# GpSimd sums the degrees of the first two pairs, pair 0 is loaded and multiplied tile by tile, the features come in six parts, and ScalarE's two loads of a piece stand apart

## What is computed

```python
h = jnp.maximum(_layernorm(x, axis=-1), 0.0)
x = x + _L0_gnn_ref(h, adj)      # (adj.T @ h) / adj.sum(axis=0)[:, None], 0 where the sum is 0
h = jnp.maximum(_layernorm(x, axis=-1), 0.0)
x = x + _L1_gnn_ref(h, adj, L1_gnn_W, L1_gnn_b)

def _L1_gnn_ref(x, adj, W, b):
    neigh1 = adj @ x
    x1 = jax.nn.swish(neigh1 @ W + b)
    neigh2 = adj @ x1
    return jax.nn.swish(neigh2 @ W + b)
```

## Time and profile before

| | us |
|---|---|
| median of 3 runs | 626.46 |
| lowest and highest run | 625.41, 627.19 |
| the profiled execution | 627.91 |
| its span in the profile | 626.1 |

### The profile page before, as it was taken

How to read it: one execution, slowest core, us unless ns; L and a number is a source line. 1 busy time by engine, 2 the same in 40 slices (tenths; PEclk the granted TensorE clock), 3 DMA queues, 4 the chain that set the end, 5 groups by cost and what they waited for, 6 DMA issues and landing times.

```text
span 626.1 us, 6939 instructions
## 1 busy us (share of the span) xinstructions
PE 609.1 (97%) x2296; PEld 413.3 (66%) x2296; DVE 541.8 (87%) x558; ACT 345.8 (55%) x456; POOL 544.2 (87%) x281
## 2 busy tenths in 40 slices
PE   8888999999999999999999999999999999999996
PEld 5355666577565567667667667777677677677774
DVE  5899699787868999897998998997998998998991
ACT  2493686595263354756656646646555546456551
POOL 2499799599688588999999989997999999998991
PEclk9999999999999999999999999999999999999999
DMA  9998999889999899999999999909999999999961
GB/s 324 382 372 301 339 320 358 293 329 275 353 351 367 287 345 334 347 347 347 347 347 348 347 348 347 283 25 220 308 348 349 348 349 348 348 348 349 348 176 34
DMA packets 151492, 197.73 MB, mean 316 GB/s; under 512 B 5280, under 2 KB 134560, under 8 KB 151456
## 3 DMA queue, kind: packets, MB, share of 16 engines
q1 hardware_dynamic: 86176, 132.92, 63.9%
...
## 4 chain that ended last, share of the span: by engine, by line
PE 63%; POOL 10%; DMA 9%; issue 6%; DVE 6%; ACT 3%; ACTq 2%; SPq 1%; POOLq 0%; DVEq 0%
PE dg L444 14%; PE dg L461 11%; PE dg L451 11%; PE dg L450 11%; DMA raw<-in_adj_dram 9%; PE m_ps L367 7%; POOL a_lo L855 5%; POOL at_lo L203 3%; PE m_ps L372 2%; PE m_ps L387 2%; PE m_ps L373 2%; DVE dg L699 2%; PE m_ps L474 2%; ACTq L285 2%; DVE turned L744 2%
## 5 line engine op out<-in xcount | busy, mean ns | idle before, releaser
L203 POOL TENSOR_TENSOR at_lo<-turned,at_hi 128x1024 fp32r<-128x1024 f32 x152 | 358.9, 2402 | 26.5 <-ACT at_hi L584 26.4
L744 DVE STREAM_TRANSPOSE turned<-raw 128x1024 f32<-128x1024 f32 x216 | 257.7, 1221 | 20.2 <-PE dg L461 13.9
L584 ACT ACTIVATE at_hi<-turned 128x1024 fp32r<-128x1024 f32 x152 | 157.0, 1055 | 97.8 <-DVE turned L744 71.1
L855 POOL TENSOR_TENSOR a_lo<-raw,a_hi 128x1024 fp32r<-128x1024 f32 x62 | 145.9, 2391 | 21.7 <-ACT a_hi L542 21.6
L699 DVE TENSOR_TENSOR dg<-raw,dg 128x2048 f32<-128x2048 f32 x60 | 137.5, 2291 | 29.2 <-DMA raw<-in_adj_dram 27.6
L450 PE MATMUL dg<-at_hi,f_hi 128*128 128x512 f32 x384 | 152.4, 397 | 0.3 <-ACT at_hi L584 0.2
L451 PE MATMUL dg<-at_hi,f_lo 128*128 128x512 f32 x384 | 151.3, 394 | 0.0
L461 PE MATMUL dg<-at_lo,f_hi 128*128 128x512 f32 x384 | 145.1, 459 | 1.2 <-POOL at_lo L203 1.2
L444 PE MATMUL dg<-turned,f_w 128*128 128x512 f32 x256 | 120.2, 592 | 0.0
L367 PE MATMUL m_ps<-raw,h 128*128 128x512 f32 x264 | 117.8, 593 | 2.5 <-DMA raw<-in_adj_dram 1.7
L461 PEld LDWEIGHTS dg<-at_lo,f_hi 128*128 128x128 f32 x384 | 72.1, 188 | 43.3 <-issue 28.9
...
## 6 DMA issues: line engine op xcount, KB each, us to landing
...
```

The lines of the kernel that those rows point to most:

```text
L203: return eng.tensor_tensor(at_lo[:, place(unit)], turned_tile(unit), at_hi[:, ring3(s)].bitcast(f32), ALU.subtract)
L584: act.activation(at_hi[:, ring3(s)], turned_tile(unit), ACT.Copy).then_inc(hi3_done, 1)
L744: dve.transpose(dst, src).then_inc(t3_done, 1)
L855: pool.tensor_tensor(a_lo[:, s % RING1], raw1[:, v % RAW1, i], a_hi[:, s % RING1].bitcast(f32), ALU.subtract).then_inc(lo1_done, 1)
```

## The change

Four things, apart from renumbering:

- **Degrees.** DVE no longer adds pairs 0 and 1. POOL sums their four tiles in `msgT`, an SBUF tile that is free then (`pool_degrees`: one instruction of 128x1024 for pair 0, two for pair 1). DVE starts with a copy of pair 2, and adds POOL's sum in `sum_degrees(0)` (one more instruction of 128x1024). ACT's first `copy_message`, which writes `msgT`, waits for that.
- **Pair 0** is loaded as two tiles of 512 KB with a semaphore each, and PE multiplies the first tile for both halves, then the second (`first_pair`).
- **Features** come in six parts of 2, 2, 4, 8, 8 and 8 tiles, ahead of the two tiles of pair 0 and of pairs 1, 3, 5 and 7. POOL's scale and shift of the last part stands behind its first `lo1`. With it, pair 8 becomes whole in quarter 0 (`WHOLE1_FIRST`), and its row pair one of those whose low part is made late.
- **ACT's blocks.** The second block of a piece is issued two units after the first.

```diff
-HEAD = ((0, 4), (4, 8), (8, 16), (16, 32))
-HEAD_PAIRS = (0, 2, 3, 4)
+HEAD = ((0, 2), (2, 4), (4, 8), (8, 16), (16, 24), (24, 32))
+HEAD_PAIRS = (0, 0, 1, 3, 5, 7)
+POOL_PAIRS = (0, 1)
-WHOLE1_FIRST = (0, 1, 2, 3, 4, 5, 7, 10, 13, 15)
-LATE_ROWS = (2, 3, 5)
-SPLIT_ROWS = (6, 8, 9, 11, 12, 14) + LATE_ROWS
+WHOLE1_FIRST = (0, 1, 2, 3, 4, 5, 7, 8, 10, 13, 15)
+LATE_ROWS = (2, 3, 5, 8)
+SPLIT_ROWS = (6, 9, 11, 12, 14) + LATE_ROWS
...
@@ SP
-                    sp.wait_ge(deg_added, back + 1)
+                    if back in POOL_PAIRS:
+                        sp.wait_ge(deg_pooled, 2 * back + 1)
+                    else:
+                        sp.wait_ge(deg_added, back + 1)
...
+            for i, ready in enumerate((tile0_loaded, raw1_loaded[0])):
+                load_head(i)
+                sp.dma_start(raw1[:, 0, i], adj_tiles[:, i, 0:QC]).then_inc(ready, 16)
+            for v in range(1, QUARTERS * PAIRS):
+                for b in head_parts(v):
+                    load_head(b)
                 load1(v)
...
@@ PE
+            def first_pair():
+
+                for i, ready in enumerate((tile0_loaded, raw1_loaded[0])):
+                    pe.wait_ge(ready, 16)
+                    pe.wait_ge(h_ready, i + 1)
+                    for half in range(2):
+                        cols = slice(half * 512, (half + 1) * 512)
+                        mm = pe.matmul(m_ps[:, cols], h[:, i], raw1[:, 0, i, cols], start=i == 0, stop=False)
+                mm.then_inc(main1_done, 1)
...
@@ ACT
                 act.wait_ge(half_done, q + 1)
+                if q == 0:
+
+                    act.wait_ge(degs_half, 1)
...
-                if unit == 1:
-                    load3(act, 3, ACT_BLOCKS)
-                if unit % QU == 0 and RAW3 <= i < len(PIECES) and i not in KEPT:
-                    load3(act, i, ACT_BLOCKS)
+                if unit in (1, 3):
+                    load3(act, 3, ACT_BLOCKS[unit // 2:unit // 2 + 1])
+
+                if unit % QU in (0, 2) and RAW3 <= i < len(PIECES) and i not in KEPT:
+                    load3(act, i, ACT_BLOCKS[unit % QU // 2:unit % QU // 2 + 1])
...
@@ DVE
-                if v % PAIRS == 0:
-                    if v > 0:
-                        dve.wait_ge(degs_ready, v // PAIRS)
+                if v == len(POOL_PAIRS):
+
+                    dve.tensor_copy(dg[:, :, :], src).then_inc(deg_added, len(POOL_PAIRS) + 1)
+                elif v % PAIRS == 0:
+                    dve.wait_ge(degs_ready, v // PAIRS)
...
+                if q == 0:
+                    dve.wait_ge(deg_pooled, 2 * len(POOL_PAIRS) - 1)
+                    step(dve.tensor_tensor(dg[:, 0, :], msgT[:, :], dg[:, 0, :], ALU.add))
...
-            head(0)
+            for b in head_parts(0):
+                head(b)
             for v in range(QUARTERS * PAIRS):
-                add_degrees(v)
-                if v < len(HEAD) - 1:
-                    head(v + 1)
+                if v not in POOL_PAIRS:
+                    add_degrees(v)
+                for b in head_parts(v + 1):
+                    head(b)
...
@@ POOL
+            def pool_degrees(v):
+
+                pool.wait_ge(raw1_loaded[v], 16)
+                if v == 0:
+                    pool.wait_ge(tile0_loaded, 16)
+                    pool.tensor_tensor(msgT[:, :], raw1[:, 0, 0], raw1[:, 0, 1], ALU.add).then_inc(deg_pooled, 1)
+                else:
+                    for i in range(2):
+                        pool.wait_ge(deg_pooled, 2 * v + i - 1)
+                        pool.tensor_tensor(msgT[:, :], raw1[:, v, i], msgT[:, :], ALU.add).then_inc(deg_pooled, 1)
+
-            for b, (lo, hi) in enumerate(HEAD):
+            for b, (lo, hi) in enumerate(HEAD[:-1]):
                 scale_shift(lo, hi, b)
+                if b - 1 in POOL_PAIRS:
+                    pool_degrees(b - 1)
...
                 lo1(v)
+                if v == splits1[0]:
+                    scale_shift(*HEAD[-1], len(HEAD) - 1)
```

More of the change, by code:

```diff
@@ L305, in store, with head_parts @@
                    .then_inc(y_out, 16)
+        def head_parts(v):
+            return [b for b in range(len(HEAD)) if HEAD_PAIRS[b] == v]
         def turned_nodes(dst, half=None):
@@ L329, in load1, with load_head @@
                   .then_inc(raw1_loaded[v % RAW1], 16)
[L331 to L335 removed]
+            def load_head(b):
+                lo, hi = HEAD[b]
+                sp.dma_start(x_rows[:, lo:hi], x_tiles[:, lo:hi]).then_inc(x_loaded[b], 16)
+            for i, ready in enumerate((tile0_loaded, raw1_loaded[0])):
[4 more added lines that the diff above has]
+                    load_head(b)
                 load1(v)
```

13 lines of the change are left out of this document (6 added, 7 removed).

## The result

| | before | after |
|---|---|---|
| median of 14 runs, us | 626.31 | 624.76 |
| lowest and highest run | 625.06, 627.23 | 623.29, 626.50 |
| the profiled execution | 627.91 | 623.29 |
| its span | 626.1 | 621.5 |

The change makes the kernel 1.55 us faster: the ratio is 0.9977, 95% interval 0.9968 to 0.9987. The forecast was 3.6 us (622.9). The time lies in the range, nearer to the first rival (625.5) than to the forecast.

A forecast was written before the change was run, and what follows sets the result against it. PE, 97% busy, bounds the kernel; its reachable idle time is in quarter 0, whose end POOL sets, then pair 9's data. 3.1 us there plus 0.5 for ACT's blocks gives 3.6: 622.9 us, range 620.3 to 626.6.

The forecast's parts named there:

- the first rival: Quarter 0: POOL or DVE runs out of spare time, 2 to 5 us of delay, gain 0 to 1.9, 625.5 us; chance 0.27.
- Two DMAs for one cost SP one more issue, far ahead of use.: Start of quarter 0: loading pair 0 as two tiles costs nothing; PE starts at 7.0 instead of 7.76, hidden by POOL's chain.
- ahead of pair 7 lie the same bytes as before: Quarter 0 loads: pair 7 lands at 31.5 and, at 2.56 us per MB, pair 9 at 36.6 instead of 37.01.
- the lower bound of 2.7 us: Quarter 0: the gain if pair 9 lands no earlier than 37.0, against 3.1 us forecast.
- What quarter 0 gives up therefore moves everything behind it forward.: From quarter 1 on: semaphore handovers carry quarter 0's whole gain, 3.1 us, to the end, DMA-bound stretches too.
- POOL's chain: Quarter 0: POOL's gapless work sets its end; with pair 8 whole, pair 9's `lo1` ends at 42.5 instead of 45.54.
- ACT's blocks, 0.5 forecast: Sweep 2: issuing the second block later removes PE's waits for the low part and ACT; 0.5 us, bounds 0 and 1.7.
- the slower rival: Sweep 2: ACT's late block sets the pace, 0.75 us a piece, 6 us lost, 629.4 on the median's scale; chance 0.09.
- The signs that I named: If right: quarter 1 near 61.9, POOL waits 1 to 2 us for pair 9, POOL's additions end by 17, shorter ACT issues.
- What frees the DMA stream: Quarter 0 loads: load 8 waits for pair 3's DVE addition at 19.9 instead of 27.5.
- The late `degs`: End of quarter 0: DVE has `degs_half` at 56.9, ACT's copy needs it about 59.3; new wait costs nothing.
- The step of `copy_nodes` behind pair 24: Around 86 us: its fourth step moves behind pair 24's `a_hi`; DVE waits about 1.5 us, within 6.7 of slack; costs nothing.

The follow-up runs named there:

- e2: The kernel before with only ACT's two blocks of a piece issued apart: 624.74 for 626.57 us, ratio 0.9967.
- e3: The kernel before with only pair 8 whole in quarter 0, its low row part made late: 625.14 for 626.57 us, ratio 0.9979.
- e6: The kernel before with ACT's blocks apart and pair 8 whole, nothing else: 622.04 for 625.95 us, ratio 0.9939.
- e1: The changed kernel, but pair 0 in one load of 1 MB and multiplied half by half as before: 622.33 for 626.57 us, ratio 0.9939.
- e4: The kernel before with only pair 0 loaded and multiplied as two tiles: 628.18 for 626.57 us, ratio 1.0028.
- e11: e6 with pair 0 loaded and multiplied as two tiles: 624.34 for 626.73 us, ratio 0.9964.
- e5: The changed kernel with pair 0's two loads cut by columns instead of tiles, multiplied half by half: 623.72 for 625.95 us, ratio 0.9966.
- e9: e8 with pair 12 whole too, its low row part late, and the feature copy begun as before: 621.17 for 626.73 us, ratio 0.9916.
- e7: e1 with all degrees added by DVE, no sums on POOL: 623.68 for 625.95 us, ratio 0.9953.
- e8: e1 with the first two feature parts joined to one of 4 tiles, five parts: 621.96 for 625.95 us, ratio 0.9938.

## Why the prediction was off

**What the parts are worth.** ACT's blocks apart -2.1 us (e2), pair 8 whole -1.3 alone and -1.75 beside it (e3; e6 against e2, 0.0028 with 0.0027 either way), six parts and POOL's degrees 0 (e1 against e6), pair 0 in two loads +1.6 to +2.4 (e4, e11, e1). The sum is between -1.0 and -2.3; measured is -1.55.

**The step that failed: "Two DMAs for one cost SP one more issue, far ahead of use."** A term of nothing stood where the runs show 1.6 to 2.4 us. The issue itself is cheap (0.45 and 0.47 us for the two tiles of pair 0 in the profile after). What the step left out is the stream: with two loads of 512 KB at its head it moves 305 to 332 GB/s from 2 to 10 us, in the four profiles with them (after, e4, e5, e11), for 345 to 374 without. The row that this could have been asked of was the earlier trace rows's 409 GB/s, taken as the pace of the stream whatever it is cut into. The next step inherits it: "ahead of pair 7 lie the same bytes as before", and so pair 9 at 36.6. The bytes were the same and the landing was 38.91. Of the 2.3 us between them, 1.4 are gone in e1 (37.49), and 0.9 were the forecast's pace: it had 9.5 us between pairs 6 and 9 (27.1 to 36.6), and e1 took 10.6. From 26 to 40 us e1 runs at 396 GB/s for 409 before, which explains 0.3 of that; the rest is open. e6, e3 and before have pair 9 at 37.02, 37.01 and 37.01, the very end (37.0) that I had kept as the lower bound of 2.7 us.

**A step that held in part: "What quarter 0 gives up therefore moves everything behind it forward."** In e3 quarter 0 gives 2.65 us and the total 1.3 (0.4 to 2.3); of e9's 1.8 us on e6 at the end of sweep 1, 0.3 are left at the first `w`. Where the rest goes is open. So the forecast's 3.1 us for quarter 0 was too much twice: by the landing of pair 9, and by counting all of it to the end.

**Two sums that don't come out**, at no cost for the forecast. Nine additions of 2.4 us from 31.9 end at 53.5 and not at 54.3 (`msgT` is added at 56.49). And delays of 2 to 5 us, each microsecond beyond the 1.7 to spare taking one off 3.6, leave 3.3 to 0.3 us and not 1.9 to 0, so the middle of the first rival is 624.7 us and not 625.5.

**Right in mechanism: POOL's chain.** Pair 8 whole removes the wait before pair 9, POOL waits for `a_hi` of pair 9 (2.36 us, forecast 1 to 2), and from there on the chain passes on what it gets, one to one: 25.4 us from `a_hi` of pair 9 to quarter 1 in six profiles (25.9 in e11, where pair 11 is waited for as well; e7 and e8 have the fall of the clock). Only its input was wrong. In e3 quarter 0 gives 2.65 us, where the lower bound was 2.7. The forecast for pair 6 with six parts (27.1) came out as 26.89 in e1. It bought nothing, since pair 9 set the chain's second half: the work had moved, as the prediction itself said, from one limit to the next.

**Mis-sized: ACT's blocks, 0.5 forecast, 2.1 measured.** The bounds were what PE visibly waits for. In the stretch from 250 to 300 us of after (answers the earlier trace rows):

```profile
DVE turned L781 <- DMA raw<-in_adj_dram: 4.1, 7, 1.4
...
PE dg L486 <- POOL at_lo L205: 0.3, 1, 0.3
```

PE's visible waits did fall by 0.9 for the low part (1.2 to 0.3), and by 0.2 for ACT. The rest came by another way. The blocked issue of 3.61 us that the earlier trace rows showed on the chain stands ahead of the table load and of `hi3`, and DVE's next step waits for that. ACT before:

```profile
287.59 3.96 ACTq L285 DMA_DIRECT2D raw<-in_adj_dram  x2
291.58 1.28 ACT L600 ACT_TABLE_LOAD   x1 [2.94 <-DVE turned L744]
```

and DVE before, behind it:

```profile
296.25 1.22 DVE L203 TENSOR_TENSOR at_lo<-dg,at_hi 128x1024 fp32r<-128x1024 f32 x1 [2.65 <-ACT at_hi L584]
...
300.80 3.46 DVE L744 STREAM_TRANSPOSE turned<-raw 128x1024 f32<-128x1024 f32 x3
```

After, ACT at the same place:

```profile
285.09 0.32 ACTq L287 DMA_DIRECT2D raw<-in_adj_dram  x1
286.17 1.28 ACT L631 ACT_TABLE_LOAD   x1
```

and DVE, which no longer waits for ACT:

```profile
291.02 1.19 DVE L205 TENSOR_TENSOR at_lo<-dg,at_hi 128x1024 fp32r<-128x1024 f32 x1
...
295.88 3.50 DVE L781 STREAM_TRANSPOSE turned<-raw 128x1024 f32<-128x1024 f32 x3 [0.26 <-DMA raw<-in_adj_dram]
```

Before, the three units at 300.80 wait for nothing that the row shows: their blocks are there, and it is DVE that is late. After, the same three wait 0.26 us for their last block: DVE is on the heels of the landings. How the lateness reaches PE is argued, not shown: a DVE that is behind frees its buffers later, and loads that are issued later land later. Of the 2.3 us, PE's waits show 1.4 before and 0.3 after; the rest lies in stretches in which PE counts as busy. The prediction read the row of the 3.61 us on the chain and gave it the price of the waits beside it. The Trainium skill, "DMA: Bandwidth & Descriptors", section "Issuing engines are not separate DMA queues", says that issuing from several engines saves only the sequencer's time, "usually small relative to the DMA itself". The trace agrees with that ratio, 2.1 us of issue in the median for 14.8 from issue to landing. But here the issuing engine has other work behind the issue, and moving the second issue was worth 2.1 us of the kernel, where the forecast by the waits had 0.5; the measurement decides.

The length of ACT's issues from 250 to 300 us, min/median/max in ns, before and after (answers the earlier trace rows; the line below it is the time from issue to landing):

```profile
L285 ACTq DMA_DIRECT2D raw<-in_adj_dram x16: 318/2106/3624, 252.7 to 294.5; - x16
...
DMA to landing us min/median/max: 13.0/14.8/16.5
```

```profile
L287 ACTq DMA_DIRECT2D raw<-in_adj_dram x17: 317/545/2447, 252.8 to 299.4; - x17
...
DMA to landing us min/median/max: 13.0/14.2/15.6
```

The median issue is down from 2.1 to 0.5 us, as forecast, though single ones still take 2.4. The time to landing didn't grow (14.2 us in the median for 14.8), and the slower rival has no trace: the whole is faster.

**The signs that I named.** Right: PE's start (6.62; 7.0 forecast), the shorter issues, the wait of POOL for pair 9. Wrong: quarter 1 (64.30; 61.9). POOL's additions end at 17.61, not by 17, because the first could start only at 8.77, when pair 0 had landed; what they cost, if anything, is within the scatter of e1 against e6 and e7. SP's waits from 0 to 60 us (answers the earlier trace rows):

```profile
SPq L334 <- PE m_ps L382: 13.6, 6, 3.9
SPq L337 <- POOL msgT L921: 5.0, 1, 5.0
SPq L337 <- DVE dg L733: 4.6, 1, 4.6
```

Those for DVE fell from 11.1 to 4.6 us (under 4 was forecast), and those for POOL's `a_lo` from 17.9 to 14.1; but 5.0 came for POOL's sum and those for PE grew from 6.3 to 13.6 (`m_ps L367` before). All together they are 37.3 us for 35.3: the slots were freed by someone else, no sooner. "What frees the DMA stream" freed nothing. One sign was badly chosen: DVE waits 4.1 us for blocks, above the 3.6 that I had called a sign of loss. It waits more because it is no longer behind; e2 has 4.3 us there and is faster.

**Steps that held at no cost.** The late `degs`: `msgT` is added at 56.49 to 57.72 us, 4.6 us ahead of ACT's copy, which waits for PE until 62.37. The step of `copy_nodes` behind pair 24: DVE waits 1.57 us for it at 87.55 (1.5 forecast), and quarter 1 takes 51.3 us as before.

**The rivals.** The time came out near the first rival, with its sum put right almost on it (624.7), but not by its mechanism: neither DVE nor POOL ran out of time (e1 has POOL and DVE do all that the change gives them, e6 nothing of it, and both have the ratio 0.9939). That e1 and e6 come out at 3.8 us, next to the forecast's 3.6, is in part luck: too much in quarter 0 (3.1 for 1.75) against too little on ACT.

**Open**: why the stream is slower with two small loads at its head. The share of busy DMA engines falls less than the bytes (0.96 and 311 GB/s in e11, 1.03 and 372 in e6), so it is not mainly a queue that runs empty. One thing more differs: SP's issue of pair 3 takes 5.33 us in e11 for 4.02 in e6, and the load behind it goes out at 10.92 us for 8.65; whether that is a cause or a result of the slower stream, no run tells. The Trainium skill, "DMA: Bandwidth & Descriptors", section "Rules for kernel authors", asks for at least 1 MiB in one DMA. That rule speaks against this part of the change and was not weighed in the prediction. The trace agrees for the first loads; sweep 2, in blocks of 512 KB throughout, keeps to 348 GB/s.
